# Retention: the per-head mean taken out of Wv, values kept without padding, the mixing bank zeroed once

## The reference, cut to what matters

```python
q = (xf @ Wq.T) ...; k = (xf @ Wk.T * SCALING) ...      # 8 heads of 16 channels
vr = (xf @ Wv.T).reshape(B, L, H, HD)                    # values, HD = 16
qk = einsum(rotated q, rotated k) * mask                  # L x L, L = 1024
qk = qk / clip(sum(abs(qk)), 1, 50000)
out = einsum(qk, vr)                                      # per head: 16 numbers a position
mu, var = out.mean(-1), out.var(-1)                       # over the 16 of a head
out = gelu((out - mu) / sqrt(var + 1e-5) * ln_g + ln_b) @ Wo.T
```

## Time and profile before

| what | value |
|---|---|
| median of 3 runs | 3769.55 us (3767.25 to 3776.1) |
| profiled execution | 3775.7 us, span 3773.8 us |
| mean granted TensorE clock | 0.861 of full |
| busy, share of the span | PE 78%, DVE 67%, ACT 46%, POOL 43% |

### The profile page before, as it was taken

One profiled execution on the slowest core, in us unless ns is written; L12 is line 12 of the kernel. 1 busy time (PEld: TensorE's weight loads), 2 busy tenths in 40 slices (PEclk: granted clock), 3 DMA queues, 4 the chain that ended last, 5 costly groups with the idle time before them and its releaser, 6 DMA issues. The chain is left out here.

```text
span 3773.8 us, 52148 instructions
## 1 busy us (share of the span) xinstructions
PE 2954.0 (78%) x14491; PEld 1342.0 (36%) x14491; DVE 2536.7 (67%) x4309; ACT 1744.0 (46%) x3385; POOL 1606.6 (43%) x1296
## 2 busy tenths in 40 slices
PE   5999999999994675477635778888799999876638
PEld 1222222222221233366523566666344443322212
DVE  4887887887882776999968766666244445544467
ACT  2887788788883554255423444445422222100000
POOL 1121121121100155699975222320477777777700
PEclk9999999999996666699966776777899999988858
DMA  8345235335311122476630010100211111001115
GB/s 262 81 136 154 58 130 162 66 118 164 83 66 63 54 80 79 140 230 208 213 97 21 29 32 30 39 21 24 69 39 41 35 35 30 19 5 5 4 56 211
DMA packets 236637, 319.91 MB, mean 85 GB/s; under 512 B 51788, under 2 KB 172684, under 8 KB 235928
## 3 DMA queue, kind: packets, MB, share of 16 engines
q1 hardware_dynamic: 206744, 296.77, 25.6%
q0 software_dynamic: 29696, 20.97, 3.1%
HBM read 170.95 MB, written 146.67 MB: 84 GB/s over the span
## 5 line engine op out<-in xcount | busy, mean ns | idle before, releaser
L1498 PE MATMUL banks<-arena 128*128 128x512 bf16 x2240 | 526.0, 388 | 105.5 <-DVE arena L2631 105.4
L959 POOL DMA_INDIRECT arena<-dst_dram,edges_now x336 | 345.9, 1029 | 102.4 <-issue 100.6
L959 POOL DMA_INDIRECT arena<-src_dram,edges_now x336 | 345.8, 1029 | 99.5 <-issue 97.4
L2148 DVE TENSOR_TENSOR arena<-banks,arena 128x512 f32<-128x512 f32 x512 | 317.5, 682 | 96.2 <-PE banks L1005 73.9
L1498 PEld LDWEIGHTS banks<-arena 128*128 128x128 bf16 x2240 | 217.6, 100 | 414.9 <-DVE arena L2631 115.9
L2148 DVE TENSOR_TENSOR keys<-banks,arena 128x512 f32<-128x512 f32 x512 | 317.5, 682 | 60.9 <-PE banks L1005 37.8
L913 POOL TENSOR_TENSOR arena<-arena 128x256 f32<-128x256 f32 x144 | 342.9, 2416 | 16.7 <-ACT arena L1808 16.5
L1686 ACT ACTIVATE arena<-arena 128x512 f32<-128x512 f32 x512 | 287.7, 619 | 130.6 <-DVE arena L2148 88.5
L2386 DVE TENSOR_TENSOR keys<-keys 128x2048 f32<-128x2048 f32 x132 | 343.6, 2642 | 1.9
L1005 PE MATMUL banks<-arena 96*128 96x512 bf16 x1024 | 282.8, 390 | 34.0 <-DVE arena L2148 31.6
L1686 ACT ACTIVATE keys<-keys 128x512 f32<-128x512 f32 x512 | 280.9, 616 | 53.5 <-PE banks L1028 46.7
(11 more groups left out here) (412 smaller groups left out, 5983.7 us busy)
## 6 DMA issues: line engine op xcount, KB each, us to landing
sorted_dram<-zeros SPq DMA_DIRECT2D x8, 8192.0 KB, 29.2
arena<-in_w SPq DMA_DIRECT2D x150, 384.0 KB, 4.0
arena<-parts_dram SPq DMA_DIRECT2D x192, 128.0 KB, 4.8
experts_dram<-keys SPq DMA_DIRECT2D x64, 256.0 KB, 2.1
keys<-experts_dram SPq DMA_DIRECT2D x8, 2048.0 KB, 8.5
parts_dram<-nodes SPq DMA_DIRECT2D x16, 768.0 KB, 3.3
slot_out_dram<-zeros SPq DMA_DIRECT2D x8, 1280.0 KB, 32.0
arena<-sorted_dram SPq DMA_DIRECT2D x150, 64.0 KB, 3.2
```

Source lines behind the costliest of these rows:

```text
L959: pool.indirect_dma_start(to[:, s, t, :], None, table[:, :], bass.IndirectOffsetOnAxis(edges_now[:, s, n, t:t + 1].bitcast(U32), 0)).then_ ...
L1498: pe.matmul(banks[:, bank, :], still[:, at + u, first * LOWS:(first + 8) * LOWS], hot[:, at + u, :], start=False, stop=False, skip_group_c ...
L2148: dve.tensor_tensor(p_slots[r % 2][:, j, :], banks[:, j, :], table[:, PER_GROUP * g + j, at:at + HALF], ALU.mult).then_inc(masked, 1)
```

## The change

- `wv` has 128 columns, 16 a head, in place of 256. The mean over each head's 16 columns is subtracted from `wv` once, on VectorE, before the first value projection. As mixing is linear over the keys and dividing is by one number a row, the mixed rows then have a mean of zero over a head's 16 channels.
- So `row_mean` and `center` go, with their semaphores `hn_mean` and `hn_centered`. Squares wait for `o_ready`. The waits in `beside` that named the dropped signals name others.
- The value matmuls have 128 moving columns, ScalarE's copies 256 columns in place of 512.
- The mix writes 16 rows of each 32-row part; the other 16 rows of bank 4 are zeroed by one matmul before the first score.

The diff, cut to its core:

```diff
-        wv = sb("wv", [P, HEADS * ROWS])
+        wv = sb("wv", [P, HEADS * KD])
+        wv_mean = sb("wv_mean", [P, HEADS])
...
-        MEAN_AT, VAR_AT, WO_AT = (13, 21, 29, 5), (17, 25, 1, 9), (7, 15)
+        VAR_AT, WO_AT = (17, 25, 1, 9), (7, 15)
...
-                    last = pe.matmul(banks[:, 6 + V_AT[n] % 2, s * 256:(s + 1) * 256], x_head[:, blk * P:(blk + 1) * P], wv[:],
+                    last = pe.matmul(banks[:, 6 + V_AT[n] % 2, s * P:(s + 1) * P], x_head[:, blk * P:(blk + 1) * P], wv[:],
...
-                    last = pe.matmul(banks[ROWS * j:ROWS * (j + 1), 4, :],
-                                     v_sb[:, a, head * ROWS:(head + 1) * ROWS], p_slots[r % 2][:, j, :],
+                    last = pe.matmul(banks[ROWS * j:ROWS * j + KD, 4, :],
+                                     v_sb[:, a, head * KD:(head + 1) * KD], p_slots[r % 2][:, j, :],
...
-            def row_mean(m, p):
-                pe.wait_ge(o_ready, m * PASSES + (p + 1))
-                pe.matmul(banks[:, 7, :], mean_16[:], o_sb[:, p, :], start=True, stop=True).then_inc(hn_mean, 1)
-
...
-                if r in MEAN_AT and (tail if r == MEAN_AT[3] else attend):
-                    p = MEAN_AT.index(r)
...
-                    row_mean(m if p == 3 else b, p)
...
-                    if p == 2 and attend:
-                        pe.wait_ge(v_ready, b * 4 + 3)
+                    if p == 2:
+                        pe.wait_ge(v_ready, b * 4 + 3) if attend else pe.wait_ge(x_mid, m * 2 - 1)
...
-                        pe.wait_ge(wo_added, m * 2 + 2) if tail else pe.wait_ge(hn_centered, b * PASSES + 1)
+                        pe.wait_ge(wo_added, m * 2 + 2) if tail else pe.wait_ge(qk_used, n * 8 + 1)
...
-                        pe.wait_ge(gn_head, (n + 1) * 4 + 3) if head else pe.wait_ge(hn_centered, b * PASSES + 2)
+                        pe.wait_ge(gn_head, (n + 1) * 4 + 3) if head else pe.wait_ge(hn_rstd, b * (2 * PASSES) + 1)
...
                     if h == 0:
-                        pe.wait_ge(hn_centered, m * PASSES + 4)
-                    elif attend:
-                        pe.wait_ge(hn_centered, b * PASSES + 1)
+                        pe.wait_ge(qk_used, n * 8 + 1) if head else pe.wait_ge(hn_rstd, m * (2 * PASSES) + 5)
                     else:
                         pe.wait_ge(hn_rstd, m * (2 * PASSES) + 7)
                     project_out(m, h)
...
             pe.wait_ge(qk_used, 8)
+            pe.wait_ge(wv_centered, 1)
             project_v(0, 0)
...
+            pe.wait_ge(zero_ready, 2)
+            pe.matmul(banks[:, 4, :], zeros16[:, 0:P], zeros16[:], start=True, stop=True)
             score(0, 0)
...
-                act.activation(v_sb[:, 2 * n:2 * n + 2, :].rearrange("p k n -> p (k n)"), banks[:, 6 + V_AT[n] % 2, :], ACT.Copy)\
+                act.activation(v_sb[:, 2 * n:2 * n + 2, :].rearrange("p k n -> p (k n)"), banks[:, 6 + V_AT[n] % 2, 0:2 * P],
+                               ACT.Copy)\
...
             def square_rows(m, p):
-                act.wait_ge(hn_centered, m * PASSES + (p + 1))
+                act.wait_ge(o_ready, m * PASSES + (p + 1))
...
-            def center(m, p):
-                dve.wait_ge(hn_mean, m * PASSES + (p + 1))
-                dve.tensor_tensor(o_sb[:, p, :], o_sb[:, p, :], banks[:, 7, :], ALU.subtract).then_inc(hn_centered, 1)
...
             head_normalise(0)
+            by_head = wv[:].rearrange("p (h e) -> p h e", h=HEADS)
+            once(dve.tensor_reduce(wv_mean[:], by_head, AX.X, ALU.add))
+            once(dve.tensor_scalar(wv_mean[:], wv_mean[:], 1.0 / KD, None, ALU.mult))
+            dve.tensor_tensor(by_head, by_head, wv_mean[:].unsqueeze(2).broadcast_to([P, HEADS, KD]), ALU.subtract)\
+                .then_inc(wv_centered, 1)
             for n in range(8):
                 rotate(0, n)
...
-    t["wv"] = head_cols(a["L0_conv_Wv"])
+    t["wv"] = a["L0_conv_Wv"].T
```

More of the change, by code:

```diff
@@ L167, in build @@
         L1 = carve([("table", HEADS * BAND), ("cos", L), ("sin", L), ("row", GROUPS * L),
-                    ("stacks", 2 * HEADS * L // 2), ("v", BLOCKS * HEADS * ROWS), ("p", 4 * HALF), ("a", 4 * HALF)])
+                    ("stacks", 2 * HEADS * L // 2), ("v", BLOCKS * HEADS * KD), ("p", 4 * HALF), ("a", 4 * HALF)])
         L2 = carve([("staged", SLOT_GROUP * EXPERT_WORDS), ("xg", SLOT_GROUP * C),
@@ L262, in build @@
         sum_step = sem("sum_step")
-        hn_mean = sem("hn_mean")
-        hn_centered = sem("hn_centered")
+        wv_centered = sem("wv_centered")
         hn_var = sem("hn_var")
@@ L1121, in beside @@
                 if head and r == 23:
-                    pe.wait_ge(hn_centered, b * PASSES + 2)
+                    pe.wait_ge(qk_used, n * 8 + 7)
                     head_mean(n + 1)
@@ L1136, in beside @@
                     if i == 2:
-                        pe.wait_ge(hn_centered, b * PASSES + 3)
+                        pe.wait_ge(x_mid, m * 2 + 1) if tail else pe.wait_ge(hn_rstd, b * (2 * PASSES) + 3)
                     project_v(n, i)
@@ L2087, in beside @@
                     rotate(n, PROJECT_AT.index(r - 1))
[L2088 to L2093, removed]
                 if tail and r - 1 in WO_AT:
```

## The result

| | before | after |
|---|---|---|
| median | 3768.4 us (3762.36 to 3776.1, 6 runs) | 3751.34 us (3747.94 to 3759.43, 6 runs) |
| profiled execution, span | 3775.7, 3773.8 us | 3750.14, 3748.3 us |
| mean granted clock | 0.861 | 0.857 |
| packets on queue q8 (instructions), whole run | 69 | 87 |

The ratio is 0.9958, 95% interval 0.9942 to 0.9975: faster by about 16 us, where 38 were forecast. The direction was right; more than half of the size is missing, and the median lies just above the stated range of 3712 to 3751 us.

What follows compares the result with a forecast made beforehand. TensorE was taken to set the pace, busy 132.3 of 139.76 us an image. Means 28.6, V 11.8, start 0.7, tail 0.9, clock -3.6 sum to 38.4: 3769.55 - 38 = 3731.5 us, range 3712 to 3751.

Steps and rivals of the forecast that it cites:

- the mean on TensorE: First stage: dropping the mean's matmul groups saves 1.19 us at each of 24 counted places, 28.6 us.
- Round 29: Mean group of round 29: no TensorE gap until round 10 of the next image, so 1.19 us stays in 8 images.
- D: TensorE merely waits for mask and abs where it had the mean; gain some 10 us, 3760 us; chance 0.03.
- A: VectorE's and ScalarE's room is used up, gaps at round 4 and behind ScalarE's bursts; 19 us lost, 3750; chance 0.08.
- B's worse half: Every gap pays two half-clock stretches, 2 us more at up to three places in half the images: 3749; chance 0.07.
- The mean of round 21: Gains nothing where TensorE then waits 1.19 us longer for VectorE's mask in round 22; counts only in image 0.
- The centring: VectorE's 32 dropped subtractions, 21.9 us of work, are worth nothing by themselves; at most a 4 us gain.
- V groups: Value projection: groups fall from 1.06 to 0.64 us, 0.42 gained at 28 places, 11.8 us (8.7 to 17).
- Mix: Mix matmuls with 16 weight columns for 32: weight loads are hidden, so gain 0, 3 us at most.
- rival C: Four 16-row mix outputs don't run side by side: 3.3 us more in 256 rounds, near 4570 us; chance 0.04.
- The term of -3.6: Longer gap of round 22 in six images prolongs TensorE's half-clock stretch behind it, costing 3.6 us.

Runs made afterwards that it cites:

- e1: Changed kernel with 32 already satisfied wait instructions ahead of TensorE's work (N = 32): 3726.89 us, ratio 0.9890 to before.
- e2: Changed kernel with 32 idle wait instructions at TensorE's head and 224 more behind the first stage: 3728.15 us, ratio 0.9887 to before.
- e7: Changed kernel with 96 idle wait instructions ahead of TensorE's work: 3720.4 us, ratio 0.9868 to before.
- e8: Changed kernel with 200 idle wait instructions ahead of TensorE's work: 3735.0 us, one run.
- e9: Repeat of e7, the changed kernel with 96 idle wait instructions ahead, in the same set as e10: 3723.23 us, ratio 0.9872 to before.
- e4: Kernel before the change with 224 idle wait instructions at TensorE's head and 32 behind the first stage: 3812.11 us, ratio 1.0110 to before.
- e5: As e1 (32 waits, mean folded into the weights), but values padded to 32 columns a head again: 3729.89 us, ratio 0.9908 to before.
- e10: As e9 (96 waits, mean folded into the weights), but values padded to 32 columns a head again: 3737.79 us, ratio 0.9915 to before.
- N = 16: Changed kernel with 16 idle wait instructions ahead of TensorE's work: 3762.1 us, one run.
- N = 0 and 256: Changed kernel with no idle wait instructions ahead of TensorE's work (after), 3751.3 us, and with 256, 3771.4 us.
- N = 228: Changed kernel with 228 idle wait instructions ahead of TensorE's work: 3754.1 us, one run.
- e11: Changed kernel with 16 idle wait instructions ahead of TensorE's work, the same run as N = 16: 3762.1 us, one run.

## Why the prediction was wrong, by its steps

**The step that failed** is the first of the mean on TensorE: "Round 29: from round 27 to round 10 of the next image there is no gap; the gain stays." Before shows none there, and with the loop in its old place there is none (e1). After has two at each of four turns, 18.1 us of waiting and 27.4 us with the clock. The sum has no term for them: I counted the instructions that go as time only, never as addresses, and none of the rivals is about instruction supply either. With this loss the sum would be 38.4 - 27.4 = 11 us of gain, and 16 were measured. Three rivals name nearly the measured time, each for a wrong reason. D (3760) has the mean's places covered by waits, and the mean groups went at their full price. A (3750) has gaps at round 4, and there are none. B's worse half (3749) has more half clock behind VectorE's and ScalarE's gaps, and in after the stretches around them (11 and 20 to 25) are 8.5 us shorter in all than in before. The stated range, 3712 to 3751, is also narrower than the plain sum of the two parts it names (18 + 5 us down, 18 + 3 up: 3708 to 3753).

**The means.** Right. In e1, stretches 12 in 8 images, 4 in 7, 28 in 8 and 20 in image 0 (the means of rounds 13, 5, 29 and 21) are each shorter by 1.18 to 1.20 us (once by 1.12, with a gap just ahead): 24 groups, 28.5 us for 28.6. After shows the same (once 0.97). The mean of round 21 in images 1 to 6 gave nothing directly: the gap behind it grew from 1.70 to 2.93.

**The centring and V.** VectorE does 108.1 us an image for 110.3, 2.2 less (forecast 2.7). V groups measure 0.64, gains of 0.43 to 0.44. Of the 28 places two kinds failed. In image 0 the gap ahead of the norm in round 28, 1.37 us in before, grew to 2.03, and the mix behind it took 1.91 us for 1.06: stretches 26 and 27 took 0.65 and 1.15 us more, where round 28 was to gain 0.42. And round 31 at the turns gave about 0 where the loop is resident (e1: +0.12 to -0.03 in stretch 30), a few tenths each. The places that can be read apart in e1 gave some 6.6 us; the six of round 26 lie in a stretch that varies by more than their 0.42. So the size of this term stays open between 3 and 20 us.

**Mix.** Right: four outputs of 16 rows run side by side, rival C is out. The Trainium skill, "TensorE: Matmul & The Clock Gate", section "What picks the tile position", asks for the full 32 partitions; the trace, 1.05 us for 1.07, does not bear that out in time. The 24 ns a load of the forecast is the row's busy time divided by its count; the row gives 114 ns as the mean of one. It changed nothing, since this term was put at 0.

**Rival A.** Out: no gap at round 4 or 14; of e1's first image below, 133.4 us, ScalarE still has 24 us left. Windows of us, then busy (instructions) of PE, PEld, DVE, ACT, POOL, granted clock, DMA share, GB/s; after, two images:

```profile
540.91:683.37 142.46, 128.17 (x714) 30.96 (x714) 108.10 (x184) 109.61 (x180) 23.67 (x16) 0.93 0.40 114
683.37:820.96 137.59, 124.85 (x713) 30.55 (x714) 108.17 (x184) 109.61 (x180) 23.67 (x16) 0.95 0.41 118
```

and e1, the same rounds:

```profile
536.29:669.65 133.36, 124.00 (x714) 30.38 (x714) 107.81 (x184) 109.54 (x180) 23.68 (x16) 0.96 0.43 121
669.65:799.73 130.08, 121.01 (x713) 29.72 (x713) 107.80 (x184) 109.55 (x180) 23.68 (x16) 0.99 0.45 124
```

e1's images are 133.4 and 130.1 us: better than the forecast's 135. In after they are 142.5 and 137.6, no shorter than before: what the rounds gained, the turn took.

**The clock.** The term of -3.6 can't be confirmed, and no run isolates it. Whether the clock falls behind a gap changes from one execution to the next: behind ScalarE's gap in round 12, stretch 11 of images 1, 2 and 4 took 4.28, 4.37 and 4.47 us in before, at a granted clock of 0.65, 0.64 and 0.62, and 2.82 us at 1.00 in e1. Stretches 11 and 20 to 25 of images 1 to 7 together should have been 1.1 us longer than in before by the forecast (3.6 for the clock, less the six value groups of round 26). They are shorter by 8.8, 3.0, 9.1, 4.8 and 5.1 us in the resident kernels e1, e2, e7, e8 and e9. But e4, with the rounds of before, is 3.8 us shorter there as well, and e5 and e10, the same rounds in two resident places, are 12.7 shorter and 3.0 longer. That is chance larger than the term.

Kernels e7 and e9, one program, came to 47.4 us (3767.8 - 3720.4) and 47.7 below before, e1 and e2 to 38.3 and 37.0. So the change with a resident loop is worth 37 to 48 us, at or above the 38 of the sum; in the profiled executions of these four the next stage starts 38.0 to 45.7 us earlier than in before's. That the sum comes out so near may be luck in part: its terms for the clock and for the values are not settled by these runs.

## What to carry to other kernels

Where an engine has a long loop of its own, look in the profile of before for its instruction packets: a queue that is silent while the loop runs says that the loop is resident. Then every instruction added to or taken from the stream ahead of it is a change of placement, which here took back more than half of what the change gains. After such an edit, look for "<-issue" gaps at the loop's turn and count the packets; if they are there, try the same kernel with a few dozen idle instructions ahead (here 32 to 96, hidden in a start where TensorE waits some 13.7 us anyway) before the change itself is blamed. When two variants are compared, compare both with their loops resident: here the placement was worth 26 us, between the mean half of the change (32 to 35 us) and the value half (7 to 16).

The lowest medians of the study are those of after with 96 waits ahead: 3720.43 and 3723.23 us in two sets, ratios 0.9868 and 0.9872 to before. Against 32 waits (0.9890 and 0.9887) that is within the intervals.

## What the runs showed of the hardware that was not expected

- TensorE's instructions come in 16,384-byte packets. A loop of some 1600 of them was either held through five images (0 packets) or fetched anew at every turn (9 packets each), decided by where it starts: N = 16 refetches, N = 32 does not. N = 0 and 256 behave alike.
- A refetching turn stopped TensorE for 2.1 to 2.8 us ahead of the score and up to 4.7 us ahead of a matmul behind it. Stretches 30 and 31 of a turn took 3 to 10 us more than before with the half clock in them: 2.8 to 3.4 with N = 228, 6.0 to 7.3 in after, 7.4 to 9.6 with N = 16.
- An instruction with two waits that are already met costs TensorE 0.109 us (23.31, 26.36 and 29.42 us to the first matmul with 200, 228 and 256 of them).
- In all the other profiled executions the later stages took less time than in before's, by 0.5 us (e4) to 17.7 us (e10, e11), in after by 10.4, though their instructions are the same. Before's profiled execution, 3775.7 us, is also the slowest but one of its six. So a difference of two single executions over the whole kernel is uncertain by that much; that was not followed up.
